# A three-layer graph network on one core: feature rows in two scaled float16 parts, counts used as one-byte numbers without a cast, and 68 instead of 64 dense blocks in the last two aggregations

## The chip, the cores and the metric

One core of one Trainium2 chip runs the whole program in one launch. The metric is the device time of that launch in microseconds. The engines of the core are named as in the profile: PE (matrix multiply; PEld is its weight load), DVE (vector), ACT (scalar), POOL (the engine that issues the indirect DMAs), SP (it issues most of the plain DMAs).

## What is computed

There are 12500 nodes with 128 features each and 400000 edges, sorted by destination; low destinations have far more edges than high ones. `segment_sum` over edges stands three times in the program.

```python
h = relu(layernorm(x))
norm = deg_inv[from_] * deg_inv[to_]
m_j = norm[:, None] * (x_j + x_j * x_i @ W1_w.T + W1_b)      # x is h here
x = x + leaky(segment_sum(m_j, to_))                          # first aggregation
h = relu(layernorm(x))
h1 = relu(h @ Ws0.T + mean(h[src] by dst) @ Wn0.T + b0)       # second aggregation
x = x + (h1 @ Ws1.T + mean(h1[src] by dst) @ Wn1.T + b1)      # third aggregation
```

## The kernel before

The nodes are padded to 98 tiles of 128. An aggregation sums, for each destination tile, the rows of a table over its edges. The kernel does that in two ways. For the first, densely populated tiles ("dense blocks") it keeps a matrix of counts: how many edges go from each source node to each of the 128 destinations. One dense block is then 98 matmuls (`product`, L1740), one for each source tile, with the 128x128 counts as weights and the table rows of that source tile (`Xp` or `Xr`, resident in SBUF) as the moving operand. One such run of 98 matmuls is called a step here. For the other tiles ("tail tiles") POOL gathers the source rows of 128 edges at a time with an indirect DMA (`gather`, L1510), DVE makes a matrix that says which edge goes to which destination (`ready`, L2051), and PE multiplies the two (`subgroup`, L1645); up to five such gathers are one subgroup.

`STEPS = (50, 64, 64)` gives the number of dense blocks in the three aggregations. The counts of the first 50 blocks are built in the first aggregation: DVE makes one-hot matrices of source and destination (`one_hots`, L2028 and L2033), PE multiplies them (`visit`, L1704), ACT evicts the counts as one-byte floats into one of two `stage` buffers (`evict`, L1289), and SP stores them (L1183). PE works on the products of block g-1 between the visits of block g. The second aggregation builds 14 more blocks in the same way (bunches of four visits at `LATE_SPOTS` in each step) and reads the other 50 back with one DMA of 1.6 MB a step (`load_c`, L1085); the third reads all. The load for step s+2 goes into the buffer of step s.

The table rows are exact to about float32. In the first aggregation a row is three bfloat16 parts of 128 columns and four columns of 1/sqrt(degree) parts and a one, 388 columns in all (`W0`). In the later two a row is two parts of 128 float32 columns, 256 in all (258 where the degree is checked), and since the counts then have to be float32 too, ACT (L1403) and DVE (L2218, L2220) cast them, 7 tiles at a time, into the ring `cast_r` of four pieces. DVE's `take` adds the parts up when it reads the bank (L2105, L2107).

The order on each engine is written out by hand: `sequence` gives the products' order, `due_at` the place of each subgroup among them, `whole_at`, `take_at`, `evicts_at` and others the slots of DVE and ACT. After the reading of a bank a tile still passes some ten "ticks" (turn, multiply with the weights, normalise, multiply again, split, store). At the end of an aggregation 11 ticks are left; some stand in its last step, others in the first step of the next. A tile's new row must be stored before the next aggregation gathers: POOL waits there for all stores (`s_pst`), and SP loads the resident rows chunk by chunk (`load_ahead`, L1157), 14 chunks of seven tiles. `Xr` lies over `Xp` and over its own earlier contents, so a chunk may be loaded only when the last step is through with it. POOL may run `RING` subgroups ahead of PE: it waits for `s_tail` (L1645).

## Time and profile before

| | us |
|---|---|
| time, median of 3 runs | 4478.44 |
| lowest and highest | 4473.98, 4479.86 |
| span of the profiled execution | 3584.4 |
| median less that span | 894.0 |
| PE busy | 3272.9 (91%) |
| PEld busy | 2796.7 (78%) |
| DVE busy | 2772.3 (77%) |
| ACT busy | 2200.0 (61%) |
| POOL busy | 2543.0 (71%) |

The span goes from the first to the last instruction; no other time of the profiled execution is known, so the part around it (894.0 us) is taken from the median. Matmuls overlap, so a busy PE says only that one was under way: the pace is read from the distance between starts. POOL's 0.30 us between two indirect DMAs is not counted as busy. In the rows of section 5 of the page stand: line, engine, operation, output and input, their shapes, xcount, busy us, mean ns of one, idle us just before, and what ended most of it.

### The profile page before, as it was taken

To read this page: it belongs to the slowest core of one execution; us is meant where nothing else is said; L and a number is where in the kernel's file an instruction comes from. 1 tells how busy PE (TensorE), PEld (TensorE's weight loads), DVE (VectorE), ACT (ScalarE), POOL (GpSimd) and SP (SyncE) were. 2 spreads that over 40 slices of the span, in tenths; PEclk is the share of its full clock that TensorE was granted. 3 is DMA by queue.
4 is the path that set the end of the run, shared out by engine and by line. 5 is a ranking of instruction groups with operands and counts; after the bars stand their busy time and mean duration, and the time that the engine had idled before them with its cause. 6 is when DMAs were issued, how large, how long until landed. Compare 5 with 4: busy or idle time off the path is not lost.

```text
span 3584.4 us, 74727 instructions
## 1 busy us (share of the span) xinstructions
PE 3272.9 (91%) x26412; PEld 2796.7 (78%) x26412; DVE 2772.3 (77%) x7631; ACT 2200.0 (61%) x4235; POOL 2543.0 (71%) x2533
## 2 busy tenths in 40 slices
PE   0069999999999999999899999999998999999998
PEld 0045666666666666666799999999998999999998
DVE  6799998988888888887467777777775777777776
ACT  1434566566666666666477777777775555555554
POOL 7717877777767777777377777676774777777775
PEclk9999999999999999999999999999999999999999
DMA  7363354555545555555877777777779777777775
GB/s 202 90 150 102 117 157 148 155 166 167 160 147 166 163 159 159 170 159 165 276 247 248 250 246 252 249 253 241 246 251 307 252 255 249 248 251 254 250 251 182
DMA packets 521514, 731.27 MB, mean 204 GB/s; under 512 B 68718, under 2 KB 459603, under 8 KB 520635
## 3 DMA queue, kind: packets, MB, share of 16 engines
q1 hardware_dynamic: 347010, 406.66, 34.7%
q0 software_dynamic: 116048, 284.86, 26.7%
q10 hardware_dynamic: 58080, 34.88, 3.3%
q8 instruction: 218, 3.57, 0.4%
q14 instruction: 158, 1.29, 0.1%
HBM read 552.54 MB, written 174.54 MB: 203 GB/s over the span
## 4 chain that ended last, share of the span: by engine, by line
PE 70%; POOL 11%; DVE 9%; issue 5%; DMA 3%; ACT 1%; SPq 0%; ACTq 0%; DVEq 0%; POOLq 0%
PE ps L1740 52%; PE ps L1704 8%; PE ps L1645 7%; POOL arena L1510 4%; POOL ring_r L1510 4%; DVE arena L2033 3%; DVE arena L2028 3%; POOL arena L1479 3%; PE ps L1680 2%; DMA ring_r<-parts,arena 2%; DMA table<-arena 1%; PE ps L1658 1%; PE ps L1670 1%; DVE arena L2105 0%; DMA arena<-parts,arena 0%
## 5 line engine op out<-in xcount | busy, mean ns | idle before, releaser
L1510 POOL DMA_INDIRECT ring_r<-parts,arena x1322 | 1305.9, 988 | 547.7 <-issue 373.4
L1740 PE MATMUL ps<-Xr,cast_r 128*128 128x256 f32 (+1 forms) x12544 | 1647.6, 286 | 11.7 <-DMA Xr<-parts 10.7
L1740 PEld LDWEIGHTS ps<-Xr,cast_r 128*128 128x128 f32 x12544 | 1552.5, 190 | 21.1 <-issue 9.7
L1289 ACT ACTIVATE arena<-ps 128x392 fp8e3<-128x392 f32 x2048 | 989.2, 497 | 599.2 <-PE ps L1704 583.6
L1403 ACT ACTIVATE cast_r<-arena 128x896 fp32r<-128x896 fp8e3 x1024 | 957.9, 951 | 593.0 <-PE ps L1740 585.8
L1510 POOL DMA_INDIRECT arena<-parts,arena x984 | 1059.0, 1076 | 318.2 <-issue 295.1
L1740 PE MATMUL ps<-arena 128*128 128x388 bf16 x4900 | 1120.9, 328 | 32.4 <-DVEq L2108 32.4
L1704 PE MATMUL ps<-arena 128*128 128x196 bf16 (+1 forms) x5550 | 1034.0, 239 | 40.5 <-DVE arena L2033 30.9
L1704 PEld LDWEIGHTS ps<-arena 128*128 128x128 bf16 x5550 | 498.7, 100 | 230.4 <-DVE arena L2033 49.8
L2028 DVE TENSOR_TENSOR arena<-arena 128x384 bf16<-128x384 bf16 (+4 forms) x1618 | 563.0, 380 | 134.7 <-PE ps L1704 129.2
L2033 DVE TENSOR_TENSOR arena<-arena 128x588 bf16<-128x588 bf16 (+4 forms) x1618 | 657.9, 438 | 0.0
L1740 PEld LDWEIGHTS ps<-arena 128*128 128x128 fp8e3 x4900 | 459.1, 97 | 235.2 <-ACT arena L1289 37.0
L2220 DVE TENSOR_TENSOR cast_r<-arena,ps 128x896 fp32r<-128x896 fp8e3 x384 | 415.9, 1085 | 218.3 <-PE ps L1740 214.5
L2218 DVE CAST cast_r<-arena 128x896 fp32r<-128x896 fp8e3 x384 | 286.7, 747 | 225.9 <-PE ps L1740 217.3
L1645 PE MATMUL ps<-ring_r,S_r 128*128 128x256 f32 x1322 | 205.7, 283 | 12.4 <-DMA ring_r<-parts,arena 12.4
L1645 PE MATMUL ps<-arena 128*128 128x388 bf16 x984 | 198.0, 329 | 15.6 <-DMA arena<-parts,arena 15.6
L1645 PEld LDWEIGHTS ps<-ring_r,S_r 128*128 128x128 f32 x1322 | 177.1, 189 | 15.4 <-issue 15.1
L1645 PEld LDWEIGHTS ps<-arena 128*128 128x128 bf16 x984 | 93.4, 97 | 69.0 <-issue 17.3
L1479 POOL DMA_INDIRECT arena<-in_dst,arena x98 | 108.1, 1103 | 30.2 <-issue 30.2
L1680 PE MATMUL ps<-w_t,arena 128*128 128x256 f32 x392 | 118.9, 385 | 8.6 <-issue 6.9
L2051 DVE TENSOR_TENSOR S_r<-arena 128x256 fp32r<-128x256 bf16 (+1 forms) x288 | 119.8, 457 | 6.1 <-PE ps L1645 5.4
L2051 DVE TENSOR_TENSOR S_r<-arena,ps 128x256 fp32r<-128x256 bf16 (+1 forms) x288 | 118.6, 453 | 0.0
(191 smaller groups left out, 1728.6 us busy)
## 6 DMA issues: line engine op xcount, KB each, us to landing
arena<-counts SPq DMA_DIRECT2D x97, 1568.0 KB
counts<-arena SPq DMA_DIRECT2D x50, 1568.0 KB
arena<-counts_late SPq DMA_DIRECT2D x27, 1568.0 KB
Xr<-parts SPq DMA_DIRECT2D x28, 896.0 KB, 12.1
counts_late<-arena SPq DMA_DIRECT2D x112, 196.0 KB
ring_r<-parts,arena POOLq DMA_INDIRECT x1322
arena<-table SPq DMA_DIRECT2D x294, 64.0 KB
arena<-parts,arena POOLq DMA_INDIRECT x984
```

The lines of the kernel that those rows point to most:

```text
L1289: act.activation(to, ps[:, unit_bank(q), 0:(b - a) * tiles].rearrange("p (n a) -> p a n", n=b - a), ACT.Copy, saturate=False).then_inc(s_e ...
L1403: act.activation(to, of, ACT.Copy).then_inc(s_castA, 1)
L1479: pool.indirect_dma_start(near[q % 7][:, t % HALF, :], None, dst.rearrange("(c e) -> c e", e=P), bass.IndirectOffsetOnAxis(ap=near_i[:, t: ...
L1510: pool.indirect_dma_start(to, None, parts_of[nth], bass.IndirectOffsetOnAxis(ap=tail_idx[:, i, first + c:first + c + 1], axis=0)).then_inc ...
L1645: t = pe.matmul(bank(b, 0, w), hots_of, rows_of, start=first + c == 0, stop=first + c == tail_visits[tail_order[nth][i]] - 1, skip_group_c ...
L1704: pe.matmul(bank(unit_bank(q), c_0, c_0 + width), hot_of_go(f)[:, c * P:(c + 1) * P], hot_of_go(f)[:, key_at:key_at + width], start=j == 0 ...
L1740: m = pe.matmul(bank(b, 0, w), counts_of, rows_of, start=e == 0, stop=e == tiles - 1, skip_group_check=True)
L2028: dve.tensor_tensor(hot_of_go(f)[:, lo * P:hi * P].rearrange("p (v f e) -> p v f e", v=v, e=2), low_of(k)[:, at_c, :].unsqueeze(2).to_broa ...
L2033: d = dve.tensor_tensor(hot_of_go(f)[:, visits * P + lo * width:visits * P + hi * width].rearrange("p (v f e) -> p v f e", v=v, e=2), key_ ...
L2051: d = dve.tensor_tensor(to[:, e + lo:e + hi, :].rearrange("p c (f e) -> p c f e", e=2), tail_rel[:, i, first + lo:first + hi, :].unsqueeze ...
L2218: dve.tensor_copy(to, of).then_inc(s_castV, 1)
L2220: dve.tensor_tensor(to, of, none_p.unsqueeze(2).to_broadcast([P, HALF, P]), ALU.add).then_inc(s_castV, 1)
```

## The change

A feature row becomes two float16 parts instead of three bfloat16 or two float32 parts. The rows are scaled by powers of two (`HIGH`, `BOTH`, and for the later two tables a bound from the norms of the weights), so that both parts stay in float16's range: the first part is the row divided by 2^11, the second what is left, and the reader of the bank weights them again. A row of the first aggregation has 2 x 129 + 2 = 260 columns, a row of the later ones still 256. The counts go to PE as the one-byte numbers they are stored as; the ring `cast_r`, its casts on ACT and DVE and PE's waits for them are gone. The second and third aggregation take 68 blocks densely, 18 of them built in the second, in five bunches of four visits a step, evicted into two stage buffers of their own and stored in one DMA each. The resident rows of the second aggregation have their own place, so chunks are loaded during the first aggregation (and those of the third during the second); three of 14 are left for the end. A load of counts now waits for the end of the products that use its buffer, not for their casts. New too are the few instructions at the start that measure and scale the weights.

```diff
-PARTS = 3
-W0 = PARTS * P + 4
 PAIR = 2 * P
+ONE = P + 1
+W0 = 2 * ONE + 2
 ROWS = PAIR + 2
+HIGH = 2.0 ** 11
+BOTH = 2.0 ** 22
...
-STEPS = (50, 64, 64)
+STEPS = (50, 68, 68)
...
-RING = (5, 3, 4)
-ONES = (5, 3, 3)
+RING = (5, 4, 5)
+ONES = 5
 HOTS = 3
-PIECES = 4
 DEEP = 5
...
-LATE_SPOTS = (10, 34, 58, 82)
+LATE_SPOTS = (8, 26, 44, 62, 80)
...
+    parts0 = nc.dram_tensor("parts0", [rows, W0], F16).ap()
+    parts1 = nc.dram_tensor("parts1", [rows, PAIR], F16).ap()
+    parts2 = nc.dram_tensor("parts2", [rows, PAIR], F16).ap()
+    counts = nc.dram_tensor("counts", [STEPS[1], loops, P, 2 * HALF * P], F8).ap()
...
+        late_stage = [view(A_BUILD + k * C_COLS, tiles, P, dt=F8) for k in range(2)]
+        Xp = view(A_X0, tiles, W0, dt=F16)
+        rows_in = [Xp, view(A_X1, tiles, ROWS, dt=F16), view(A_X0, tiles, PAIR, dt=F16)]
+        ring = view(A_RING, RING[0] * CHUNKS, W0, dt=F16)
+        ring_pairs = view(A_RING, max(RING[1:]) * CHUNKS, PAIR, dt=F16)
+        S = view(A_S, ONES * CHUNKS, P, dt=BF16)
...
+        ahead_at = [{}, {}]
+        for nth in range(2):
+            behind = 14 if nth == 0 else 12
+            for e, c in enumerate(chunk_order[nth]):
+                due = rank_at[nth].index(chunk_rank[nth][c]) + behind
+                ahead_at[nth].setdefault(due if due < 2 * STEPS[nth] - 2 else None, []).append(e)
...
-                casts_of_step(sp, nth, s - 2)
+                sp.wait_ge(s_agg, steps_before[nth] + s - 1)
...
+                if g >= GROUPS:
+                    sp.wait_ge(s_counts[(g - GROUPS) % 2], stored_blocks((g - GROUPS) % 2, g - GROUPS + 1))
+                sp.dma_start(in_runs(stage[k]), counts[g].rearrange("c p e -> p c e")).then_inc(s_c[k], 16)
+            def store_late(g):
+                sp.wait_ge(s_evict, evicts_of[g])
+                sp.dma_start(counts[g].rearrange("c p e -> p c e"), in_runs(late_stage[(g - GROUPS) % 2])).then_inc(s_counts[(g - GROUPS) % 2], 16)
...
-                    products_of(sp, piece_of[1, STEPS[1] - 1, e])
+                    sp.wait_ge(s_agg, steps_before[1])
...
-                if nth == 1 and len(under[c]):
-                    n = max(first_freed.index(b) for b in under[c])
-                    if n < halves - 1:
-                        sp.wait_ge(s_piece, n + 1)
-                    else:
-                        sp.wait_ge(s_agg, steps_before[1])
-                sp.dma_start(Xr[:, c * HALF:(c + 1) * HALF, 0:PAIR].bitcast(F32),
+                    sp.wait_ge(s_tailrel, 2)
+                sp.dma_start(rows_in[nth][:, c * HALF:(c + 1) * HALF, 0:PAIR],
...
+                            for e in ahead_at[0].get(j, []):
+                                load_ahead(1, e)
...
-            def second_part(n):
...
-                act.activation(Xp[:, n * HALF:(n + 1) * HALF, P:2 * P], rest[:, n % 2], ACT.Copy).then_inc(s_two, 1)
+            act.wait_ge(s_normps, 1)
+            act.activation(norms[:, 4:7], bank(7, 0, 3), ACT.Sqrt)
+            act.activation(norms[:, 7:8], norms[:, 3:4], ACT.Sqrt).then_inc(s_normed, 1)
...
-                    act.activation(split_r[:, n % 3, 0:P], bank(7, 0, P), ACT.Copy)
+                    act.activation(split[:, n % 3, 0:P], bank(7, 0, P), ACT.Copy, scale=1.0 / HIGH)
...
-                def cast_piece(g):
-                    to, of = cast(act, g)
-                    act.activation(to, of, ACT.Copy).then_inc(s_castA, 1)
...
+                            pool.wait_ge(s_tail, subs_before[nth])
...
-                if nth == 0:
-                    counts_of, rows_of = stage[k][:, a, :], Xp[:, a, 0:w]
-                else:
-                    counts_of, rows_of = cast_r[:, piece_of[nth, s, e // HALF] % PIECES * HALF + e % HALF, :], Xr[:, a, 0:w]
-                m = pe.matmul(bank(b, 0, w), counts_of, rows_of, start=e == 0, stop=e == tiles - 1, skip_group_check=True)
+                m = pe.matmul(bank(b, 0, w), stage[k][:, a, :], rows_in[nth][:, a, 0:w], start=e == 0, stop=e == tiles - 1, skip_group_check=True)
                 if e == tiles - 1:
                     m.then_inc(s_agg, 1)
-                elif e % HALF == HALF - 1 and (nth or last):
-                    m.then_inc(s_piece, 1)
...
-                dve.tensor_tensor(rest[:, n % 2], tout[:, n % 2, :, 0:P], Xp[:, a:b, 0:P], ALU.subtract).then_inc(s_rest, 1)
...
-                dve.tensor_tensor(Xp[:, a:b, 2 * P:3 * P], rest[:, n % 2], Xp[:, a:b, P:2 * P], ALU.subtract).then_inc(s_split0, 1)
...
+                dve.tensor_copy(Xp[:, a:b, P:P + ONE + 1:ONE], dinv_parts[:, a:b, :])
+                dve.scalar_tensor_tensor(Xp[:, a:b, ONE:ONE + P], Xp[:, a:b, 0:P], -HIGH, tout[:, n % 2, :, 0:P], ALU.mult, ALU.add).then_inc(s_split0, 1)
...
-                    then(dve.tensor_reduce(agg, bank(b, 0, PARTS * P).rearrange("p (k f) -> p f k", k=PARTS), AX.X, ALU.add))
-                else:
-                    then(dve.tensor_reduce(agg, bank(b, 0, PAIR).rearrange("p (k f) -> p f k", k=2), AX.X, ALU.add))
...
+                    of = sums[:, r % SUMS, 0:ONE]
+                    d = dve.tensor_scalar(of, bank(b, ONE, 2 * ONE), 1.0 / HIGH, None, ALU.mult)
+                    if t < GROUPS:
+                        d = dve.tensor_tensor(agrees[:, t:t + 1], bank(b, 2 * ONE, 2 * ONE + 1), degree[:, t:t + 1], ALU.is_equal)
+                    then(d)
+                    then(dve.tensor_tensor(of, bank(b, 0, ONE), of, ALU.add))
+                    dve.sem_inc(s_free if t < STEPS[nth] else s_freet, 1)
...
+                then(dve.scalar_tensor_tensor(to, bank(b, 0, P), rdegs[:, 2 * nth - 2, t:t + 1], tin[:, i3 % DEEP, :], ALU.mult, ALU.add))
+                then(dve.scalar_tensor_tensor(to, bank(b, P, PAIR), rdegs[:, 2 * nth - 1, t:t + 1], to, ALU.mult, ALU.add))
+                dve.sem_inc(s_free if t < STEPS[nth] else s_freet, 1)
...
-                def cast_piece(g):
-                    to, of = cast(dve, g)
-                    if stream[g][0] == 1:
-                        dve.tensor_copy(to, of).then_inc(s_castV, 1)
-                    else:
-                        dve.tensor_tensor(to, of, none_p.unsqueeze(2).to_broadcast([P, HALF, P]), ALU.add).then_inc(s_castV, 1)
```

On PE, in the middle of the second aggregation, before (each row is an instruction in program order; L1645 is a subgroup, L1740 a product, L1704 a visit, L1670 and L1680 the two multiplications of a tile's tick):

```order
L1704 MATMUL ps<-arena 128x196 x4
L1740 MATMUL ps<-Xr,cast_r 128x256 x24
L1704 MATMUL ps<-arena 128x196 x4
L1740 MATMUL ps<-Xr,cast_r 128x256 x19
L1645 MATMUL ps<-ring_r,S_r 128x256 x5
L1740 MATMUL ps<-Xr,cast_r 128x256
L1670 MATMUL ps<-ident,arena 128x128
L1680 MATMUL ps<-w_t,arena 128x256
```

The same place in the changed kernel (L1580 subgroup, L1667 product, L1639 visit, L1605 and L1615 the tick's):

```order
L1639 MATMUL ps<-arena 128x196 x4
L1667 MATMUL ps<-arena 128x256 x18
L1639 MATMUL ps<-arena 128x196 x4
L1667 MATMUL ps<-arena 128x256 x17
L1580 MATMUL ps<-arena 128x256 x5
L1667 MATMUL ps<-arena 128x258 x9
L1605 MATMUL ps<-ident,arena 128x128
L1615 MATMUL ps<-w_t,arena 128x256
```

A bunch of four visits now comes every 18 products, not 24; the products are as wide as before.

On POOL, the end of the first and the start of the second aggregation, before (L1510 is a gather of 128 rows, L1487 fetches edge records for the counts):

```order
L1510 DMA arena<-parts,arena 128x388 x42
L1487 DMA arena<-records,first_edge 128x256
L1510 DMA arena<-parts,arena 128x388 x101
L1487 DMA arena<-records,first_edge 128x256 x2
L1510 DMA ring_r<-parts,arena 128x256 x30
```

and in the changed kernel (L1444, L1421):

```order
L1444 DMA arena<-parts,arena 128x260 x42
L1421 DMA arena<-records,first_edge 128x256
L1444 DMA arena<-parts,arena 128x260 x101
L1421 DMA arena<-records,first_edge 128x256 x2
L1444 DMA arena<-parts,arena 128x256 x25
```

In the first aggregation the gathers are as many as before, 984, each row 260 columns of two bytes instead of 388. In the later two they are 1150 in all instead of 1322.

On SP, the end of the first aggregation, before (L1157 loads a chunk of resident rows, L1085 counts, L1105, L1106 and L1108 rows for one tile):

```order
L1105 DMA arena<-table 128x128 [waits s_x1]
L1106 DMA arena<-in_x 128x128
L1157 DMA Xr<-parts 128x7x256 [waits s_visit,s_pst2,s_piece,s_pst1,s_pst0]
L1157 DMA Xr<-parts 128x7x256 [waits s_pst2,s_piece,s_pst1,s_pst0] x2
L1157 DMA Xr<-parts 128x7x256 [waits s_pst2,s_pst1,s_pst0]
```

and in the changed kernel (L1101, L1055, L1056, L1058):

```order
L1055 DMA arena<-table 128x128 [waits s_x1]
L1056 DMA arena<-in_x 128x128
L1101 DMA arena<-parts 128x7x256 [waits s_pst2,s_pst1,s_pst0] x3
L1058 DMA arena<-table 128x128 [waits s_pst1,s_pst2,s_pst0,s_u,s_counts1,s_counts0]
```

Before, all 14 chunks follow here; now three do, and eleven stand earlier in the queue.

## Rows read from the trace of the kernel before

**Rows 1.** Windows of the first and second aggregation: span, busy us (x instructions), clock, DMA, GB/s
```profile
275.00:1729.00 1454.00, 1380.76 (x10709) 950.83 (x10708) 1228.56 (x4023) 898.77 (x2175) 1094.81 (x1014) 0.99 0.53 158
1729.00:2717.00 988.00, 974.65 (x8145) 955.41 (x8144) 724.54 (x2018) 736.92 (x1363) 684.67 (x666) 1.00 0.75 248
```

**Rows 2.** The page, section 5 (its columns are explained above)
```profile
L1740 PE MATMUL ps<-Xr,cast_r 128*128 128x256 f32 (+1 forms) x12544 | 1647.6, 286 | 11.7 <-DMA Xr<-parts 10.7
...
L1740 PE MATMUL ps<-arena 128*128 128x388 bf16 x4900 | 1120.9, 328 | 32.4 <-DVEq L2108 32.4
...
L1740 PEld LDWEIGHTS ps<-arena 128*128 128x128 fp8e3 x4900 | 459.1, 97 | 235.2 <-ACT arena L1289 37.0
...
L1645 PE MATMUL ps<-ring_r,S_r 128*128 128x256 f32 x1322 | 205.7, 283 | 12.4 <-DMA ring_r<-parts,arena 12.4
L1645 PE MATMUL ps<-arena 128*128 128x388 bf16 x984 | 198.0, 329 | 15.6 <-DMA arena<-parts,arena 15.6
```

**Rows 3.** Timeline of PE in the first aggregation: start us, length us, instruction
```profile
1000.17 0.25 PE L1704 MATMUL ps<-arena 128*128 128x196 bf16 x1
1000.26 0.49 PE L1740 MATMUL ps<-arena 128*128 128x388 bf16 x2
1000.59 0.24 PE L1704 MATMUL ps<-arena 128*128 128x196 bf16 x1
```

**Rows 4.** Chain, last aggregation: start us, us, matmuls
```profile
2841.77 4.41 PE ps L1740 x37
2846.18 0.46 PE ps L1645 x4
```

**Rows 5.** Windows for line L1510 on POOL, one stretch of each aggregation
```profile
400.00:1600.00 1200.00, 890.79 (x853) 0.99 0.53 158
1900.00:2600.00 700.00, 495.81 (x483) 1.00 0.75 249
2850.00:3500.00 650.00, 491.76 (x520) 1.00 0.78 252
```

**Rows 6.** Waits of POOL, 400 to 1600 us: total us, times, longest us
```profile
POOL arena L1510 <- PE ps L1645: 20.7, 15, 16.4
```

**Rows 7.** DVE by form, 400 to 1600 us (columns as section 5)
```profile
L2105 DVE TENSOR_REDUCE arena<-ps 128x128 f32<-128x384 f32 x83 | 45.2, 544 | 0.0
...
L2133 DVE SCALAR_TENSOR_TENSOR arena<-bias,s0b,ps 128x128 f32<-128x128 f32 x85 | 29.0, 342 | 11.7 <-PE ps L1658 11.7
```

**Rows 8.** Windows, early first aggregation; then POOL's timeline there
```profile
320.00:340.00 20.00, 18.14 (x145) 12.15 (x144) 20.00 (x64) 7.46 (x15) 15.80 (x8) 1.00 0.16 43
...
331.00 16.60 POOL L1510 DMA_INDIRECT arena<-parts,arena  x1 [2.37 <-PE ps L1645]
```

**Rows 9.** Timelines at the stage ends: POOL, then PE
```profile
1693.27 0.94 POOL L1510 DMA_INDIRECT arena<-parts,arena  x1 [0.30 <-issue]
...
1746.83 0.94 POOL L1510 DMA_INDIRECT ring_r<-parts,arena  x1 [49.93 <-DMA table<-arena]
...
1729.07 1.76 PE L1740 MATMUL ps<-Xr,cast_r 128*128 128x256 f32 x10
...
2717.03 2.18 PE L1740 MATMUL ps<-Xr,cast_r 128*128 128x256 f32 x16 [0.32 <-issue]
```

**Rows 10.** PE's timeline at a late gather, and windows around it
```profile
599.54 1.78 PE L1645 MATMUL ps<-arena 128*128 128x388 bf16 x5 [6.28 <-DMA arena<-parts,arena]
...
597.00:604.00 7.00, 4.46 (x26) 2.79 (x26) 1.10 (x2) 1.61 (x4) 5.48 (x6) 0.55 0.57 172
```

**Rows 11.** SP's timeline, one load of counts; windows eight us later
```profile
2936.78 0.37 SPq L1085 DMA_DIRECT2D arena<-counts  x1
...
2943.00:2944.00 1.00, 1.00 (x11) 1.00 (x10) 0.72 (x1) 0.89 (x2) 0.70 (x2) 1.00 1.06 364
...
2945.00:2947.00 2.00, 2.00 (x20) 2.00 (x18) 1.75 (x6) 1.23 (x2) 1.44 (x2) 1.00 0.42 129
```

**Rows 12.** Chain, second aggregation: start us, us, matmuls
```profile
2342.17 0.35 PE ps L1704 x4
```

More of the change, by code:

```diff
@@ L327, in program @@
         rdeg = sb("rdeg", [P, tiles])
+        rdegs = sb("rdegs", [P, 4, tiles])
+        norms = sb("norms", [P, 16])
         dinv = sb("dinv", [P, tiles])
@@ L405, in program @@
         tout = view(A_RING, 2, HALF, ROW0)
-        rest = view(A_RING + 2 * HALF * ROW0, 2, HALF, P)
-        below = view(A_RING + 2 * HALF * (ROW0 + P), HALF, P, dt=BF16)
+        below = view(A_RING + 2 * HALF * ROW0, HALF, P, dt=BF16)
+        squares = view(A_S, 4, P)
         place = [A_L]
@@ L421, in program @@
         near_i = part(tiles, dt=I32)
-        dinv4 = part(tiles, 4, dt=BF16)
+        dinv_parts = part(tiles, 2, dt=F16)
         mv = part(tiles, 2)
@@ L462, in program @@
         yS = part(3, 2 * P)
-        split = part(3, PAIR)
-        split_r = view(place[0] - 3 * PAIR, 3, PAIR, dt=F32R)
+        split = part(3, PAIR, dt=F16)
         assert place[0] <= arena_cols
@@ L1163, in last_step @@
                     load_next(nth, j)
-                for e in range(halves):
+                for e in ahead_at[nth].get(None, []):
                     load_ahead(nth + 1, e)
@@ L1200, in _ @@
                             load_next(nth, j)
+                            for e in ahead_at[1].get(j, []) if nth == 1 else []:
+                                load_ahead(2, e)
                         if nth == 1:
-                            for n in (2 * (s - LATE_FROM) - 1, 2 * (s - LATE_FROM)):
-                                if 0 <= n < late_stores:
-                                    store_run(n)
+                            for g in range(GROUPS, STEPS[1]):
+                                if built_at[g] + 1 == s:
+                                    store_late(g)
                         if s + 2 < STEPS[nth]:
@@ L1398, in tick @@
                     deviation(nth, j)
-                def cast_piece(g):
-                    to, of = cast(act, g)
-                    act.activation(to, of, ACT.Copy).then_inc(s_castA, 1)
-                for g in range(PIECES):
-                    if not by_vector[g]:
-                        cast_piece(g)
                 for j in range(2 * GROUPS - 2, places[0]):
@@ L1410, in _ @@
                 for g in range(len(stream)):
-                    if g >= PIECES and not by_vector[g]:
-                        cast_piece(g)
                     for nth, j in whole_at.get(g, []):
@@ L1573, in _ @@
             pe.matmul(bank(6, P, 3 * P), ones_r[0:1, :], bias_r.rearrange("p k f -> p (k f)"), start=True, stop=True).then_inc(s_prepared_pe, 1)
+            pe.wait_ge(s_squares, 1)
+            pe.matmul(bank(7, 0, 3), ones_r[:, :], norms[:, 0:3], start=True, stop=True).then_inc(s_normps, 1)
             def degrees(go):
@@ L1642, in subgroup @@
                 for c in range(count):
-                    one, row = (m % n * CHUNKS + c for n in (ONES[nth], RING[nth]))
-                    hots_of, rows_of = (S[:, one, :], ring[:, row, 0:w]) if nth == 0 else (S_r[:, one, :], ring_r[:, row, :])
-                    t = pe.matmul(bank(b, 0, w), hots_of, rows_of, start=first + c == 0, stop=first + c == tail_visits[tail_order[nth][i]] - 1, skip_group_check=True)
+                    one, row = (m % n * CHUNKS + c for n in (ONES, RING[nth]))
+                    rows_of = (ring if nth == 0 else ring_pairs)[:, row, :]
+                    t = pe.matmul(bank(b, 0, w), S[:, one, :], rows_of, start=first + c == 0, stop=first + c == tail_visits[tail_order[nth][i]] - 1, skip_group_check=True)
                 t.then_inc(s_tail, 1)
@@ L1809, in _ @@
                         if i in turn_at[nth]:
[L1810 removed]
+                            so_far = max([q for q in range(len(units)) if unit_groups[q][0] >= GROUPS and spot_of(visits_to[q] - 1) <= (s, e)], default=None)
                             pe.wait_ge(s_evict, evicts_of[GROUPS - 1] if so_far is None else evicts_to[so_far])
@@ L1975, in scales @@
                 own(dve.reciprocal(rdeg[:, :], root))
+                for k in (1, 3):
+                    own(dve.tensor_scalar(rdegs[:, k, :], rdeg[:, :], norms[:, 12 + k:13 + k], None, ALU.mult))
                 dve.sem_inc(s_root_in, 1)
@@ L2199, in _ @@
                         tail_columns(1)
+                    if f == hots_before_batch[2]:
+                        for k in range(4):
+                            dve.tensor_scalar(rdegs[:, k, :], rdeg[:, :], norms[:, 12 + k:13 + k], None, ALU.mult)
                     for j in take_before.get(f, []):
```

328 lines of the change are left out of this document (122 added, 206 removed).

## The prediction

> **What bounds the kernel now.** I read the windows first, then the groups of PE and POOL, then the chain and the timelines, to learn which engine sets the pace in which aggregation. I call the stretches A (275 to 1729 us, first aggregation), B (to 2717) and C (to the end); their borders are the first products of each [rows 9]. In B PE is busy for 975 of 988 us [rows 1]. In C the chain is products and subgroups without a gap: 37 products in 4.41 us, 119 ns each, 4 matmuls of a subgroup in 0.46 us [rows 4]. So B and C are PE's.
>
> A looks like PE's too, 1381 of 1454 us [rows 1], but POOL's rows say more. Of the 984 gathers of A, 853 lie between 400 and 1600 us and take 890.8 us [rows 2, 5], 1.04 us each; with the 0.30 us that follows each, 1.35 us, they fill 1150 of 1200 us. POOL's waits for PE there are 20.7 us [rows 6], the rest goes to fetching edge records. POOL is thus as good as saturated in A. PE and POOL run side by side at nearly the same pace, and only one of them gets quicker by the change. In C, too, a gather every 1.25 us (650 us by 520 [rows 5]) is just what PE's pace needs.
>
> **What a matmul costs after.** In A two matmuls of 388 columns take 0.33 us from start to start [rows 3], 0.425 ns a column. One of 260 columns is then 0.111 us, one of 256 columns 0.109 us. The float32 products of B and C have 256 columns and take 0.119, so something besides the columns costs them 10 ns. I take 0.109: in A one-byte counts are loaded as weights already, a load takes 97 ns on average [rows 2], less than 109; and visits, with two-byte weights, come 0.09 us apart [rows 3]. The unseen case is a one-byte load behind a matmul of only 109 ns; the ends are 0.109 and 0.119.
>
> The Trainium skill, "TensorE: Matmul & The Clock Gate", section "Weight-path perf modes", says that the fast weight load is on for 128 weights whose type is not float32. By it the 10 ns of B and C are the float32 load and go away; if the row's 119 ns stayed, the sum below would be 145 us higher. The trace agrees as far as it goes: 0.425 ns a column with one-byte weights, more only with float32.
>
> **A, part by part.** PE: 4900 products and 984 gathered matmuls [rows 2] lose 128 columns, 54 ns: 320 us of work. DVE: reading a bank was a reduce of 544 ns and a short one, and becomes two operations of 129 columns from PSUM; the nearest such costs 342 ns [rows 7], together 684: no change, so DVE keeps its 1229 us of 1454. POOL: the same 984 gathers. Neither the number of rows nor POOL's work on each changes; C's gathers move 1024 bytes a row and take 0.95 us (491.8 by 520), A's move 776 and take 1.04 [rows 5], so bytes don't set the price. Hence the 320 us are hidden behind POOL, and PE will wait for gathers. What A does lose:
> - POOL's waits for PE go: 20 us [rows 6].
> - The end. The last gather of A ends at 1694.2 and B's first product starts at 1729.1 [rows 9], 34.9 us later, since PE is behind with a last step of 98 products. With PE ahead, the last step starts earlier and is bound by its gathers, then by the chain of ticks through PE, ACT and DVE. Ends: 8 us (a landing and the last tenth of a step) and 35; I take 14, minus 21.
> - The start: the split loses one pass of 896 columns on DVE for each seven tiles, 14 in all, 1.2 us each by the 544 ns for 384 columns [rows 7], at most 17 us; most of it lies beside the indirect DMAs that fetch destinations. I take 4. The new work on the weights' norms falls into the same cover; without it, it would be some ten small operations, 3 us.
> - Two losses. DVE will have fewer pauses, and between 320 and 340 us, where it is busy for all 20, only 8 gathers pass and one takes 16.6 us [rows 8]. Ends: nothing, and rival 2; I take 10 us. And PE's clock: after the wait of 6.28 us at 599.5 the granted clock over seven us is 0.55, so at its lower level of 1.2 GHz for nearly all of them [rows 10]. PE has 54 ns x 120 = 6.5 us to spare in a step of 28, which takes most of that up. I take 5.
>
> A: -20 - 21 - 4 + 10 + 5 = -30 us.
>
> **B.** Products: 64 x 98 = 6272 at 0.119 is 746 us, 68 x 98 = 6664 at 0.109 is 726: -20. Gathered matmuls: 661 at 0.119 to 575 at 0.109: -16. Visits: 256 more (four blocks of 64) at 0.35 us for four [rows 12]: +22. ACT and DVE lose their casts, which nothing waits for. POOL needs 575 x (495.8/483 + 0.30) = 763 us of B's 975, so it no longer matters. The restart: POOL's first gather of B comes 17.8 us after B's first product [rows 9], because all rows must be stored first, and that stays. Five gathers and a landing later, at 26 us, PE can go past place 150, which it reaches at 16 us of products and 5 of ticks: +5. B: -9 us.
>
> **C.** Products -20, gathered matmuls -16, as in B. C lasts 867 us, and 6272 and 661 matmuls at 0.119 are 825: 42 us are lost in the first step, in short waits for gathers, and after the last matmul. The resident rows are now loaded ahead, so PE no longer stands for them; but the restart 16 us after the start [rows 9] leaves 9 us at place 150, the counts of the third step some 3, the end 13: 25 instead of 42, -17. POOL needs 575 x 1.25 = 719 us of 814. C: -53 us.
>
> The counts' loads: now a load can start only at the end of the step whose buffer it takes. A load issued at 2936.8 keeps the DMA engines full until after 2944, and by 2945 to 2947 they are at 0.42 [rows 11]: 8 to 9 us. A step of C becomes 98 x 0.109 + 8.5 x 0.109 = 11.6 us. That hides the load, with 2.6 us to spare.
>
> **Sum.** Span 3584.4 - 30 - 9 - 53 = 3492; the profiled execution's own time isn't known, so I add the 894 us by which the median exceeds its span: 4386 us. A difference of 0.2%, 9 us, is about what can be told from none.
>
> **Rivals.**
> 1. A is not held by POOL. For it: PE is nearly as busy. Then DVE would be next, with its 1229 us and about 6% of waits for itself, A 1305 instead of 1424: 4267 us. Against it: POOL has 20.7 us of slack in 1200.
> 2. Gathers get dearer in A, the case that ends slower. DVE's one-hot operations crowd into less time and hold POOL off as between 320 and 340 us, 2.5 us for a gather. If a tenth of the 984 went that way, it would be 98 x 1.15 = 113 us: 4386 - 10 + 113 = 4489. It decides where the mean of a gather in A rises by 102/984, 0.10 us, to 1.45. Against it: a PE that waits for POOL leaves DVE's buffers full, and DVE pauses. The Trainium skill, "SBUF — State Buffer", tells of a port pair that VectorE and GpSimd take for a whole instruction, one blocking the other; that speaks for this rival.
> 3. Products stay at 0.119 us: 13328 + 1150 matmuls x 10 ns = 145 us: 4531. It decides at 0.115.
> 4. The counts come late in C. If they need 12.6 us, 66 steps wait 1 us each: 4452. For it: the casts used to free the buffer some three pieces early.
>
> **Chances.** The forecast 0.58 (its own range 4350 to 4425), rival 1 0.11, rival 2 0.13 (half of it below 4450), rival 3 0.05, rival 4 0.05, mixtures 0.08. The range 4310 to 4450 leaves out rival 1 and the upper parts of 2, 3 and 4. Faster by over 0.2%: 0.58 + 0.11 + 0.09 + 0.03 + 0.07 = 0.88; within 0.2%: 0.03; slower: 0.09 (3 and the rest of 2).
>
> **What would show it.** In the profile after: A's products some 27 us a step and A about 1424 us; POOL's only idle time between gathers there 0.30 us, and PE with waits of one to five us for gathers, with short stretches at the lower clock; products of B and C 0.109 us apart; C without a wait of PE for counts; steps of C 11.6 us. Wrong if gathers in A are quicker or slower than 1.35 us apiece, if the 894 us around the span move, or if a wait for counts stands in C.

## The result and the profile after

The changed kernel took 4336.1 us (median of 4 runs, 4321.2 to 4341.7) where the kernel before took 4479.2 us (4474.0 to 4486.2): ratio 0.966, interval 0.963 to 0.969, 143 us faster. The prediction was 4386 us, 92 us faster. The page of the changed kernel and its windows for A, B and C (columns as in [rows 1]; the gather is now line L1444, the product L1667, the visit L1639, ACT's eviction L1236, a one-hot pair L1968 and L1973, a gathered matmul L1580):

```profile
span 4329.9 us, 74600 instructions
PE 3263.8 (75%) x27286; PEld 2656.2 (61%) x27286; DVE 2080.9 (48%) x7045; ACT 1295.0 (30%) x3331; POOL 2325.4 (54%) x2364
PEclk9998788888888878788898999999999899999999
L1444 POOL DMA_INDIRECT arena<-parts,arena x2134 | 2142.1, 1004 | 1616.1 <-PE ps L1580 815.2
```
```profile
315.00:2246.00 1931.00, 1345.47 (x10706) 1041.66 (x10704) 1234.09 (x4021) 859.41 (x2172) 1075.13 (x1014) 0.83 0.34 97
2246.00:3410.00 1164.00, 1008.04 (x8716) 850.46 (x8715) 480.90 (x1863) 357.06 (x983) 567.73 (x582) 0.95 0.54 173
3410.00:4330.00 920.00, 830.74 (x7245) 705.08 (x7242) 167.45 (x546) 2.17 (x8) 546.03 (x576) 0.98 0.57 180
```

This is not the profile that the prediction forecast. Its execution took 4331.6 us, so 1.7 us lie outside the span and not 894; A lasts 1931 us and not 1424; and POOL, which the prediction held to be saturated there, is busy for 1075 of them and waits 815 us for PE over the whole kernel. Either the change did something strange, or the profile of before was of another kind of execution than its timed runs. The experiments settle which: every kernel here runs at one of two levels. The kernel before takes 4474 to 4531 us at the long level and 3579 to 3596 us at the short one, and runs made one after the other on one chip are all at one level (chip 9 at the long one, chips 1, 5 and 6 at the short one; for the result above and for the profile of before no chip is known). The profile of before that was read (span 3584.4) is of the short level, its median of the long one. So the changed kernel has two results, and they agree: 0.966 at the long level, and 0.970 (0.968 to 0.972) and 0.973 (0.972 to 0.974) in two sets of runs at the short one, 3480.8 us against 3585.0 and 3492.5 against 3588.8. Comparisons below are made within a level.

The short level can be held against the rows of the prediction. Windows for A, B and C of the changed kernel there:

```profile
span 3487.9 us, 74600 instructions
```
```profile
268.00:1722.00 1454.00, 1156.26 (x10708) 976.66 (x10706) 1214.18 (x4020) 873.25 (x2173) 1126.43 (x1014) 0.92 0.46 129
1722.00:2682.00 960.00, 954.51 (x8712) 844.15 (x8710) 480.93 (x1862) 359.26 (x982) 561.89 (x582) 1.00 0.66 210
2682.00:3488.00 806.00, 793.65 (x7247) 709.64 (x7244) 165.97 (x546) 2.16 (x8) 544.07 (x576) 0.99 0.65 205
```

Against [rows 1] A lasts as long as before, 1454 us, although PE's work in it fell by 225 us. B is 28 us shorter and C, 867 us before, is 61 us shorter. With 7 us at the start the span is 96.5 us shorter, where 92 were forecast.

### The profile page after: what moved, and what is told of

Its sections match the earlier page's. It is cut to its first block, busy times and chain, and to the rows that moved or that the text cites. A ratio compares the mean times of both kernels' runs of the same rounds, so it can differ in the third digit from the quotient of the medians.

```text
span 4329.9 us, 74600 instructions
## 1 busy us (share of the span) xinstructions
PE 3263.8 (75%) x27286; PEld 2656.2 (61%) x27286; DVE 2080.9 (48%) x7045; ACT 1295.0 (30%) x3331; POOL 2325.4 (54%) x2364
## 4 chain that ended last, share of the span: by engine, by line
PE 64%; issue 12%; another core or an unknown queue 10%; DVE 7%; ACT 4%; POOL 1%; DMA 0%; SPq 0%; ACTq 0%; DVEq 0%; POOLq 0%
PE ps L1667 43%; PE ps L1639 12%; PE ps L1580 5%; ACT arena L1236 3%; DVE arena L1973 2%; DVE arena L1968 2%; PE ps L1615 2%; PE ps L1593 1%; PE ps L1605 1%; SPq L1021 0%; ACT arena L1192 0%; PE ps L1625 0%; DVE arena L1987 0%; POOL arena L1413 0%
## 5 line engine op out<-in xcount | busy, mean ns | idle before, releaser
L1444 POOL DMA_INDIRECT arena<-parts,arena x2134 | 2142.1, 1004 | 1616.1 <-PE ps L1580 815.2
L1667 PE MATMUL ps<-arena 128*128 128x256 f16 (+2 forms) x18228 | 2662.7, 283 | 162.0 <-issue 110.7
L1667 PEld LDWEIGHTS ps<-arena 128*128 128x128 fp8e3 x18228 | 1816.2, 101 | 472.7 <-issue 176.9
L1639 PE MATMUL ps<-arena 128*128 128x196 bf16 (+1 forms) x5806 | 1111.1, 256 | 641.0 <-issue 329.7
L1236 ACT ACTIVATE arena<-ps 128x392 fp8e3<-128x392 f32 x2176 | 1022.4, 499 | 1575.6 <-PE ps L1639 929.2
L1639 PEld LDWEIGHTS ps<-arena 128*128 128x128 bf16 x5806 | 568.3, 107 | 878.2 <-issue 511.7
L1968 DVE TENSOR_TENSOR arena<-arena 128x384 bf16<-128x384 bf16 (+4 forms) x1746 | 596.8, 375 | 745.0 <-PE ps L1639 449.4
L1973 DVE TENSOR_TENSOR arena<-arena 128x588 bf16<-128x588 bf16 (+4 forms) x1746 | 698.4, 433 | 0.0
L1987 DVE TENSOR_TENSOR arena<-arena 128x256 bf16<-128x256 bf16 (+1 forms) x924 | 253.3, 319 | 760.7 <-remote 460.9
L1580 PE MATMUL ps<-arena 128*128 128x256 f16 (+1 forms) x2134 | 345.5, 294 | 6.7 <-issue 5.9
L2056 DVE SCALAR_TENSOR_TENSOR arena<-ps,rdegs,arena 128x128 f32<-128x128 f32 x196 | 68.5, 349 | 392.7 <-remote 243.9
L1580 PEld LDWEIGHTS ps<-arena 128*128 128x128 bf16 x2134 | 218.4, 105 | 46.3 <-issue 7.7
L1421 POOL DMA_INDIRECT arena<-records,first_edge x42 | 59.0, 1405 | 245.1 <-PE ps L1548 202.2
L1615 PE MATMUL ps<-w_t,arena 128*128 128x256 f32 x392 | 134.3, 427 | 6.6 <-issue 3.4
L1248 ACT ACTIVATE arena<-ps 128x256 f32<-128x256 f32 x196 | 76.3, 389 | 0.0
L1615 PEld LDWEIGHTS ps<-w_t,arena 128*128 128x128 f32 x392 | 68.8, 218 | 8.9 <-issue 6.6
L2057 DVE SCALAR_TENSOR_TENSOR arena<-ps,rdegs,arena 128x128 f32<-128x128 f32 x196 | 68.8, 351 | 6.9
```

Of the source, the lines that this page charges most:

```text
L1236: act.activation(to, ps[:, unit_bank(q), 0:(b - a) * tiles].rearrange("p (n a) -> p a n", n=b - a), ACT.Copy, saturate=False).then_inc(s_e ...
L1248: act.activation(yS[:, n % 3, :], bank(7, 0, 2 * P), ACT.Copy).then_inc(s_yS, 1)
L1444: pool.indirect_dma_start(to, None, parts_of[nth], bass.IndirectOffsetOnAxis(ap=tail_idx[:, i, first + c:first + c + 1], axis=0)).then_inc ...
L1580: t = pe.matmul(bank(b, 0, w), S[:, one, :], rows_of, start=first + c == 0, stop=first + c == tail_visits[tail_order[nth][i]] - 1, skip_gr ...
L1615: pe.matmul(bank(7, 0, 2 * P), hT[:, r % 2, :], w_t[:, 2 * nth + 1:2 * nth + 3, :].rearrange("p k f -> p (k f)"), start=True, stop=True).t ...
L1639: pe.matmul(bank(unit_bank(q), c_0, c_0 + width), hot_of_go(f)[:, c * P:(c + 1) * P], hot_of_go(f)[:, key_at:key_at + width], start=j == 0 ...
```

## Experiments

**1. The kernel before, once more.**

> The kernel before, unchanged, to have a profile of an execution like the timed ones. Theory 1 (the one of the prediction): the 894 us by which the timed executions exceed the profiled span lie outside the span, so the span is again about 3584 us with a mean granted clock near 0.99, and stretch A again lasts about 1454 us with PE busy for 95% of it. Theory 2: the profile that the prediction read was of an execution unlike the timed ones; then this profile has a span within 10 us of its own time of about 4479 us, a mean clock near 0.9, and stretch A of 2000 to 2300 us, in which PE has many waits of 1 to 6 us and drops to the lower clock behind them, as in the profile of the changed kernel (A 1931 us at a mean granted clock of 0.83).

It took 4531.4 us with a span of 4529.7 (the kernel before beside it 4502.8). Its windows for A, B and C:

```profile
327.00:2346.00 2019.00, 1574.40 (x10704) 1004.29 (x10702) 1240.08 (x4022) 876.02 (x2175) 1061.51 (x1014) 0.89 0.38 114
2346.00:3456.00 1110.00, 1025.91 (x8145) 974.71 (x8143) 717.87 (x2017) 726.58 (x1363) 711.97 (x666) 0.98 0.68 221
3456.00:4530.00 1074.00, 904.75 (x6939) 864.45 (x6939) 611.10 (x976) 469.99 (x520) 625.96 (x662) 0.96 0.63 201
```

Theory 2 holds. DVE, ACT and POOL are busy as long as in [rows 1], to some 4%; PE is busy longer at its lower clock. What is added is above all waits, and they lie in all three stretches, not around the span. At this level the change takes 88 us from A, adds 53 to B and takes 153 from C, by one profile of each.

**2. The changed kernel, unchanged, at the short level,** in two sets of runs.

> The changed kernel, unchanged. The kernel before took 4479 us in the runs shown and 3590 us beside the last four kernels, whose spans were 1.7 us below their own times, so the times depend on the chip, and not on 894 us outside the span. If this chip is one on which the kernel before takes some 3590 us, the prediction's sum holds without the 894 us: a span of 3480 to 3500 us, A 1450 us with PE waiting for gathers, B 961 to 980, C 803 with steps of 11.6 us, ratio 0.970 to 0.975. If it is one on which the kernel before takes some 4480 us, then again 4320 to 4340 us, ratio 0.966, with A 1931, B 1164 and C 920 us. Rival for the first case: the long steps of B (28 to 31 us at steps 12, 18, 25, 31 and 37) stand there too, and B takes 1030 us or more.

> The changed kernel, unchanged, beside the run with wide products in A. Where the kernel before takes some 3585 us: 3481 us again, ratio 0.970, A 1454 us, with some 37 waits of PE for gathers in A and 25 gathers of over 2 us between 400 and 1600 us. Where the kernel before takes some 4480 us: 4336 us, with A 1931, B 1164, C 920 us.

3480.8 and 3492.5 us; A 1454 and 1465 us, B 960 and 960, C 806 and 804. The waits of PE and POOL from 400 to 1600 us (total, times, longest), and POOL's line L1444 in the window 400 to 1600:

```profile
POOL arena L1444 <- issue: 253.7, 832, 0.3
PE ps L1580 <- DMA arena<-parts,arena: 152.5, 37, 7.3
```
```profile
400.00:1600.00 1200.00, 904.66 (x843) 0.91 0.47 133
```

POOL's one wait that comes to anything is the 0.30 us behind each gather, and PE waits for landings, 152 us where it was 15.6 in the kernel before: the profile that the prediction asked for. But 843 gathers pass in those 1200 us where [rows 5] has 853, and a gather costs 1.07 us, not 1.04. In C the chain has 56 or 57 products in 6.11 or 6.22 us between the five gathered matmuls, 0.109 us each, and from the fourth step on a step takes 11.1 to 11.8 us:

```profile
2999.97 0.33 PE ps L1667 x3
3000.30 0.55 PE ps L1580 x5
3000.84 6.11 PE ps L1667 x56
```

**3. No gathers in A and C,** but for those of the first five subgroups of each; PE's waits for them are left out too, and its matmuls take old rows. Run twice.

```diff
-                for c in range(count):
+                for c in range(count if nth == 1 or m - subs_before[nth] < 5 else 0):
...
-                pe.wait_ge(s_gather[m % RING[nth]], 16 * gathered_to[m])
+                if nth == 1 or m - subs_before[nth] < 5:
+                    pe.wait_ge(s_gather[m % RING[nth]], 16 * gathered_to[m])
```

> The changed kernel without the gathers of A and C except for those of the first five subgroups of each: the matmuls and one-hot matrices of all subgroups stay and take old rows; B is as it was. It leaves out about 960 of 984 gathers in A and 550 of 575 in C. Theory 1, the prediction's, that POOL's gathers set A's pace: A falls from 1931 us to 1400 or less. Theory 2, that POOL waits for PE in A of the timed executions (815 us of waits for PE): A stays within 40 us of 1931. For the stall of about 0.8 us that PE has after every subgroup of C: if it is the landing of the rows or POOL's and the DMA's work beside it, it goes with the gathers and C falls from 920 us to about 820; if it comes from PE's own queue or from the semaphores of PE, it stays and C does not move by more than 20 us.

> The changed kernel without about 960 of A's 984 gathers and 550 of C's 575 (their matmuls stay and take old rows; B is as it was). Where the kernel before takes some 3590 us: again A 1287 us, bound by DVE, and 3322 us in all. Where it takes some 4480 us: theory 1, A is bound there by the stalls and the lower clock of PE and not by POOL, so A stays within 60 us of 1931 us; rival, POOL's or the DMA's work beside PE makes the stalls, and A falls below 1700 us. In C PE has there a stall of 0.8 us after every subgroup: if it comes with the gathers, C falls from 920 to about 810 us; if it is PE's own, C stays within 20 us of 920.

Both were at the short level: 3323.3 and 3328.6 us. A and C of the first:

```profile
268.00:1555.00 1287.00, 1099.43 (x10710) 940.67 (x10709) 1202.27 (x4021) 873.62 (x2173) 62.11 (x55) 0.99 0.30 97
2517.00:3322.00 805.00, 792.39 (x7251) 709.35 (x7248) 163.09 (x548) 2.17 (x8) 20.28 (x22) 0.99 0.50 160
```

A falls by 167 us: the gathers are what holds A of the changed kernel. DVE is then busy for 1202 of 1287 us, near where rival 1 of the prediction had it (1305); that DVE is the next bound is read from this share and was not tested. C does not move: its gathers are hidden. What the gathers do at the long level was not seen.

**4. Wide rows in A and C.**

```diff
+                more = 388 if nth == 0 else 280 if nth == 2 and s >= 2 else 0
+                if more and a < tiles - 1:
+                    at_col = a * (W0 if nth == 0 else PAIR)
+                    row, w = flat_in[nth][:, at_col:at_col + more], more
```

> The changed kernel with its products widened again: 388 columns instead of 260 in A (all but every 98th product; the gathered matmuls stay at 260), 280 instead of 256 in C from its third step on, so that a product costs again what it did before; the added columns are neighbouring rows, and nobody reads them. It adds 4850 x 54 = 262 us of PE work to A and about 6400 x 10 = 64 us to C. Theory 1, that PE's columns were hidden in A behind something else: A lasts 1931 us plus at most 90. Theory 2, that PE's lower clock takes back what the columns save: PE busier in A keeps its clock, the mean granted clock of A rises from 0.83 to about 0.89, and A lasts 1990 to 2040 us, as in the kernel before. Theory 3, that PE's work sets A's time: plus 262 us. For C: if the gain of 151 us there is the cheaper product, C gets 64 us longer and the rest, some 90 us, came from the casts that went; if a stall in PE's queue hides the columns, C does not move.

3535.5 us, at the short level. C takes 867 us, 61 more than with 256 columns, nearly the 64 of ten nanoseconds a product: C is bound by products and they cost by columns, one-byte weights or not. A, with 262 us more of columns, got shorter, 1438 against 1454 us. That was expected by none of the three theories.

**5. Wide rows in A alone,** to see whether this was chance (with the fetches of experiment 7, which do nothing at this level).

```diff
+                if nth == 0 and a < tiles - 1:
+                    w = 388
+                    row = flat_in[:, a * W0:a * W0 + w]
```

> The changed kernel with products of 388 columns instead of 260 in A alone (the added 128 are neighbouring rows that nobody reads), and with the later fetches of edge records. Theory 1: in A, where POOL sets the pace, PE's wider products cost nothing, and PE that waits less keeps its clock and lets DVE's one-hot operations come evenly, so that gathers cost 1.04 us instead of 1.07; A falls from 1454 us to some 1438, as in the run with wide rows in A and C (its A 1438), and the kernel takes 3460 to 3470 us where the kernel before takes 3585, ratio 0.966 against 0.970 of the changed one. Where the kernel before takes some 4480 us, the fetches bring 60 to 80 us in B, and A moves by less than 40 us. Rival: the 16 us of A in that one run were chance; then 3481 us, as the changed kernel.

3471.6 us, ratio 0.967 (0.966 to 0.968), beside the unchanged changed kernel at 0.973 (0.972 to 0.974): 21 us less for 262 us of useless work. Its window for A, and its line L1445 (the gather) in 400 to 1600 us:

```profile
267.00:1703.00 1436.00, 1338.69 (x10704) 957.70 (x10702) 1222.24 (x4020) 892.64 (x2172) 1093.05 (x1014) 0.98 0.46 131
```
```profile
400.00:1600.00 1200.00, 889.91 (x863) 0.98 0.48 135
```

POOL is busy for 1093 us in A and not 1126 (1140 in the changed kernel beside it), for the same 1014 instructions: a gather costs 1.03 us again. The time of A follows POOL's busy time here and not PE's.

Why is a gather dearer when PE is quicker? The changed kernel has 26 gathers of over 2 us in A after 400 us (30 in its second set of runs); the kernel before has 5 and this one 4. Between 400 and 1600 us they are 25 with a mean of 3.1 us, and the other gathers are even cheaper than before, 1.01 us against 1.04. One of the long ones, in POOL's timeline of the changed kernel at the short level, and what DVE does meanwhile:

```profile
1136.05 1.03 POOL L1444 DMA_INDIRECT arena<-parts,arena  x1 [0.30 <-issue]
1137.39 3.89 POOL L1444 DMA_INDIRECT arena<-parts,arena  x1 [0.31 <-issue]
1141.58 0.94 POOL L1444 DMA_INDIRECT arena<-parts,arena  x1 [0.30 <-issue]
```
```profile
1136.18 0.83 DVE L1973 TENSOR_TENSOR arena<-arena 128x588 bf16<-128x588 bf16 x2
1136.93 0.96 DVE L1987 TENSOR_TENSOR arena<-arena 128x256 bf16<-128x256 bf16 x4
1137.80 0.62 DVE L1968 TENSOR_TENSOR arena<-arena 128x384 bf16<-128x384 bf16 x2
1138.34 0.83 DVE L1973 TENSOR_TENSOR arena<-arena 128x588 bf16<-128x588 bf16 x2
1139.09 0.62 DVE L1968 TENSOR_TENSOR arena<-arena 128x384 bf16<-128x384 bf16 x2
1139.63 0.83 DVE L1973 TENSOR_TENSOR arena<-arena 128x588 bf16<-128x588 bf16 x2
1140.38 0.34 DVE L2072 SCALAR_TENSOR_TENSOR arena<-bias,s0b,ps 128x128 f32<-128x128 f32 x1
1140.88 0.35 DVE L2074 SCALAR_TENSOR_TENSOR arena<-arena 128x128 f32<-128x128 f32 x1 [0.16 <-DVE arena L2072]
```

DVE builds one-hot matrices in bf16 without a pause from 1136.2 to 1140.4, and the gather that was issued in it ends at 1141.3, 0.56 us after DVE's first free moment at 1140.7. Of the 25 long gathers 22 end 0.55 to 0.56 us after the start of such a pause, and 25 of the 27 in the second set of runs. A row of operations alone isn't enough: over a hundred gathers lie wholly under lines L1968 and L1973 in either kernel (128 before, 123 after) and take 1.08 us in both. What changed is the rhythm. DVE waited for PE 143 times between 400 and 1600 us before, for 116 us in all, and waits 65 times now, for 156: fewer and longer waits, with longer rows of work behind them.

The Trainium skill, "SBUF — State Buffer", describes a lock on a port pair that VectorE or GpSimd holds for a whole instruction while the other blocks; the trace agrees with the blocking and shows one gather held off by a whole row of instructions.

**6. Two buffers for the one-hot matrices, not three,** so that DVE can run ahead of PE by less.

```diff
-HOTS = 3
+HOTS = 2
```

> The changed kernel with two buffers for one-hot matrices of visits instead of three, so that DVE can run ahead of PE by one group less. Theory 1, that gathers of A are dearer than before because DVE, let go after one of PE's waits, builds several groups without a pause and holds POOL off: between 400 and 1600 us the gathers that lie for 90% or more under DVE's one-hot operations fall from 25 or 27 to under 12, their mean falls from 2.4 or 2.6 us to under 1.6, and the mean of all gathers from 1.07 or 1.08 to 1.05 us or less; what PE then waits longer for DVE (45 us before) may take back the gain. Rival: the long gathers come from something else, such as the fetches of edge records or DMA traffic; then the mean stays at 1.07 to 1.08 us and A gets longer by PE's waits for DVE alone.

3510.9 us, ratio 0.978 (0.976 to 0.980). The window of L1444 from 400 to 1600 us, and the waits there; the first line is DVE's in the changed kernel:

```profile
400.00:1600.00 1200.00, 854.53 (x830) 0.95 0.47 132
```
```profile
DVE arena L1968 <- PE ps L1639: 156.1, 65, 6.6
```
```profile
DVE arena L1968 <- PE ps L1639: 147.1, 128, 5.1
PE ps L1639 <- DVE arena L1973: 127.2, 143, 2.7
PE ps L1625 <- DVE arena L1946: 95.5, 25, 4.5
POOL arena L1444 <- PE ps L1580: 58.1, 33, 21.8
```

DVE waits twice as often as in the changed kernel, for less time each, and the gathers of over 2 us are 6, not 25: a gather takes 1.03 us. That half of theory 1 is shown. (The trace does not give the counts and means that the expectation names for gathers lying for 90% under DVE's operations; those of over 2 us are what can be counted.) POOL's busy time in A falls by 81 us to 1045, half of it before 400 us, but PE now waits 127 us for the matrices of its visits (45 in the changed kernel) and 96 for DVE's line L1946 (13 there), and A takes 1464 us. The bursts make gathers dear, and the third buffer is still worth having.

**7. The fetches of edge records for the late blocks, two steps later,** twice.

```diff
-        ... if due_at[1][n] >= (turns[k - 2] + 2) * tiles): k for k in turns if k - 2 in turns}
+        ... if due_at[1][n] >= (turns[k - 2] + 4) * tiles): k for k in turns if k - 2 in turns}
```

> The changed kernel, with POOL's fetches of edge records for the late blocks two steps of B later in POOL's order, so that POOL does not stand at them while PE has not yet read the records before. Theory: in the changed kernel steps 12, 18, 25, 31 and 37 of B take 28.5 to 30.7 us instead of 15.5, because POOL waits up to 19 us at such a fetch and the gathers behind it come late. Then these five steps fall to about 16 us, POOL's wait for the records' transposes goes from 98 us to under 20, B from 1164 to about 1100 us, and the kernel takes some 4270 us. Rival: the long steps come from the late blocks' own building (records, keys, one-hot matrices), which the place of the fetch does not touch; then B and the total do not move by more than 10 us.

> The changed kernel with POOL's fetches of edge records two steps of B later in POOL's order. Where the kernel before takes some 3590 us POOL did not wait at the fetches long enough to be late for PE: same time as the changed kernel within 10 us (3482 us). Where it takes some 4480 us, PE is slower than POOL and POOL meets the fetch early: the five long steps of B shrink by 12 to 14 us each, and the kernel takes 60 to 80 us less than the changed one. Rival: the long steps come from building the late blocks, and nothing moves on either chip.

3482.1 and 3479.4 us at the short level, where the five long steps of B do not exist: no change, which tells nothing of the long level. There the theory has in the meantime a strong point against it: in B the gathers behind the first subgroup are issued 18.6 us or more ahead of their matmuls, so POOL's waits at the fetches (98.5 us) make nothing late. The five long steps, some 70 us of B, are unexplained.

**8. 64 dense blocks, as before, with all else of the change.**

```diff
-STEPS = (50, 68, 68)
+STEPS = (50, 64, 64)
```

> The changed kernel with 64 dense blocks in the later two aggregations, 14 of them built late, as before; all else of the change stays. By the prediction's prices the four blocks bring B 64 us less work on gathered rows and add 43 us of products and 22 of visits, so the kernel should be within 10 us of the changed one in B, and some 20 us slower in C, about 4350 us. Rival: in the profile of the changed kernel a step of B still takes 17.1 us, as long as in the kernel before, so what B does per step and not what it does per row sets its time; then four steps less are worth 68 us in B and some 54 in C, against 87 gathered matmuls more in each, and the kernel is 50 to 90 us faster than the changed one, 4250 to 4290 us.

3488.4 us at the short level, ratio 0.972 (0.970 to 0.973), the changed kernel 0.970 and 0.973, and 0.969 and 0.971 with the fetches of experiment 7: no difference. Its windows for B and C, and PE's wait from 2650 to 3450 us:

```profile
1719.00:2627.00 908.00, 899.14 (x8139) 792.35 (x8138) 421.78 (x1637) 302.94 (x851) 654.84 (x666) 1.00 0.67 214
2627.00:3486.00 859.00, 777.09 (x6945) 680.23 (x6943) 171.69 (x588) 2.16 (x8) 627.97 (x662) 0.98 0.61 192
```
```profile
PE ps L1580 <- DMA arena<-parts,arena: 69.7, 53, 2.8
```

Four blocks more cost 52 us in B (960 against 908) and bring 53 in C (806 against 859). They bring so much in C because 661 gathers at 1.25 us are 826 us: with products at 0.109 us and 64 blocks C would be POOL's, and PE waits for landings. Neither theory of the expectation had POOL in it. The 52 us of B are PE's work: 392 products at 0.109 us are 43, 256 visits 22, less 9 for 86 gathered matmuls at 0.109; the first theory had put 64 where the 9 stand.

**9. Fewer signals.** Of PE's visits only those for whose end somebody waits add to the semaphore.

```diff
-                          ...).then_inc(s_visit, 1)
+                if w + 1 in told_by:
+                    t.then_inc(s_visit, 1)
```

> The changed kernel, where not each of PE's 5806 visits adds one to the semaphore on which ACT and DVE wait, but only those visits for whose end somebody waits, about half. The order and the work stay. Theory 1: a signal costs nothing, and A and B do not move by more than 10 us. Theory 2, for a chip on which the kernel before takes some 4480 us: PE's stalls come from handing on its signals; half of them gone takes at least 100 us out of A (1931 us) and 30 out of B (1164 us), and leaves C.

3485.5 us, ratio 0.972 (0.970 to 0.974), A 1455 us: leaving out half of the signals brings nothing at the short level. No run of it was at the long one.

## Why the prediction came out as it did

The time lies in the range given, but not by the sum, and two of the prediction's own signs of being wrong came true: the 894 us moved to 1.7, and gathers in A are slower than 1.35 us apiece (1.07 and 0.30). By its own steps, at the level of its rows (3584.4 to 3487.9 us):

- **"The profiled execution's own time isn't known, so I add the 894 us by which the median exceeds its span": wrong.** Nothing lies around the span; the median was of executions in which the waits within it are longer. The forecast gain of 92 us is that of the short level (97 by the profiles, 96 to 104 by the medians); at the long level it was 143, and that it was of like size is no merit of the sum.
- **A is POOL's: right, and the columns were hidden.** Without gathers A is 167 us shorter; with 262 us of columns more it is not longer. Of the -30 us nothing came within A. The waits of POOL's gathers for PE fell from 23.0 to 9.6 us in A (-13 for -20). The end shrank as forecast: from the end of A's last gather to B's first product 15.6 us instead of 34.9 (-19 for -21). But POOL is busy for 32 us more (forecast +10), which takes back both. The failed term is the price of a gather, rival 2 at some 0.3 of its strength (32 of 113 us): with a PE that waits for POOL, DVE does pause, as its "against" said (156 us between 400 and 1600 us, 116 before), but in fewer and longer waits, and it works in bursts behind them.
- **PE's clock** was at its lower level of 1.2 GHz for longer than before: 222 us of A against 27, 0.92 in the mean against 0.99. PE waited 5.87 us for a landing from 1322.5 on, and from 1326 to 1333 the granted clock was 0.51. What of it reaches A's end (+5 forecast) cannot be told from the gathers' price, since wide rows mend both; two buffers had cheap gathers at 0.95 and other waits.
- **B, -9: came out at -28.** PE's busy time fell by 20 us (974.7 to 954.5; forecast -14), and its idle time from 13 to 6 us. The restart, put at +5, cost nothing: the first two steps take 15.5 and 15.4 us, 17.0 and 17.7 before.
- **C, -53: came out at -61.** Products at 0.109 us (rival 3 is out), steps of 11.1 to 11.8 us, and no wait for counts (rival 4 is out). All 7239 matmuls at 0.109 are 789 us, so 17 us are lost around them where the forecast put 25.
- **The start, -4: came out at -7.**

At the long level the short level's account does not hold. PE's queue there stands again and again: from 3500 to 4300 us of the changed kernel PE is busy for 737 of 800 us, where the short level has all 700 of 700 from 2750 to 3450. The waits from 3500 to 4300 us:

```profile
POOL arena L1444 <- remote: 147.7, 96, 1.7
PEld ps L1667 <- issue: 99.0, 171, 1.3
```

"Remote" and "issue" say that the profile has no releaser. The kernel before has the same standstills in a tighter weave: from 3550 to 4480 us PE is busy for 799 of 930 us, with 43.6 us of waits of PE for DVE's casts, 41.1 of its loads for ACT's, and 274 of DVE's casts for PE. That would explain why C gained 153 us there and not 61: without casts PE, ACT and DVE no longer wait for each other behind a standstill. This is argued from one profile of each kernel and not shown by an experiment.

## What to carry to other kernels

Before a profile is trusted for a sum, hold its span against the timed runs; where they differ by more than a few us, profile the kernel again, because stages may have other bounds in the timed executions. Where POOL gathers and DVE builds matrices, the time follows what a gather costs beside DVE, and work taken from PE can make it dearer: try a version with that work left in. More dense blocks pay in the stage where gathers bound the pace and cost as much in the one where products do.

## What the runs showed of the chip

- The same code had two levels, 25% apart (4479 and 3585 us), with runs made together at one of them. The durations of single instructions barely differ: in the kernel before a gather of the later aggregations takes 988 ns at the short level and 1008 at the long one, a one-hot operation of line L2033 438 and 442. Waits are added, on every engine, and PE's lower clock comes with them (0.89 and 0.83 in A, 0.99 and 0.92 at the short level).
- In the later two aggregations nine of ten gathers land 2.1 to 6.0 us after their start at either level. At the long one, behind the first subgroup of each aggregation, they start 10.3 us or more ahead of their matmuls in the kernel before and 18.6 or more in the changed one, so they are not what PE waits for.
- The trace of the kernel before holds 78,700 updates of semaphores at the short level and 32,652 at the long one, for the same instructions. The Trainium skill, "NOTIFIC — the notification-queue block", section 7.1, says that a full queue of records can stall the engine that writes it, in one of its modes; in that mode no record is dropped, and here updates are missing, which does not speak for it. The long level was seen with a known chip on chip 9 alone, the short one on three others. Whether it is the chip, the taking of records or something else is open; no run here tells.
- 262 us of matmul columns that nobody needs made a kernel 21 us faster (3492.5 to 3471.6 us). With them gathers cost 1.03 us in place of 1.08 and PE's clock in A rose from 0.92 to 0.98; no run tells the two apart.
